# A macaron block: the route stage's row maxima, low parts and normalising are moved between engines and places

## The chip, the cores and the metric

The kernel runs on one core of one Trainium2 chip. A core has TensorE (PE: matrix products, transposes as products with an identity), VectorE (DVE), ScalarE (ACT), GpSimd (POOL) and SyncE (SP), which issues the DMAs. Each engine works through its own list of instructions in order, and semaphores tie the lists together. The metric is the time of one execution in microseconds (us) on the device. Before the change the median of 3 runs is 1989.15 us (1987.82 to 1989.57).

## The reference

The block is ffn, attention, ffn. Each ffn is a soft mixture of experts; its first part, the route, is what the change touches:

```python
x = L0_attn_x                                   # (4, 2048, 256)
x = x + 0.5 * ffn(layernorm(x))
x = x + attention(layernorm(x))
x = x + 0.5 * ffn(layernorm(x))

def ffn(x, ...):                                # E, S = 16, 64 -> 1024 slots
    x = layernorm(x) * g + b
    se = layernorm(slot_embeds) * scale
    logits = einsum('bnd,esd->bnes', x, se)
    dispatch = softmax(logits, axis=1)          # over the tokens
    combine = softmax(logits over all slots)    # over experts and slots
    slots = einsum('bnd,bnes->besd', x, dispatch)
    ... experts (gate, up, down), then combine @ eout
```

## The kernel before

There are three stages per ffn, each with its own names in the profile: route (f1r, f2r), experts (f1e, f2e) and combine (f1c, f2c); attention (at) stands between the two ffns. The banks of PSUM are f1bank and f2bank.

The route works by batches (4), each of four groups of 512 tokens (four tiles of 128); the 1024 slots are eight chunks of 128, or two halves of 512. A product in full precision is made of three products of high and low parts, so a token tile, its transpose and the exponentials are each split into `hi` (a copy that rounds) and `lo` (the difference).

`emit(b, fill, drain)` writes the work of one batch for one engine. Fill is for batch b: token statistics (VectorE), normalising (GpSimd, line 380), the transposes of the tokens (TensorE, line 681, "T"), their high parts (ScalarE, line 587) and low parts (VectorE, line 444), the logits as eight chunks of six matmuls (lines 692 to 694, `mm(0)` to `mm(7)`), their eviction with a bias (ScalarE, line 596), the maximum of each slot over tokens (VectorE, line 466), the maximum of each token over chunks (lines 459 and 456), and its last step, the transposes of that row maximum (TensorE, line 701) with a reduction (line 479). Drain is for batch b − 1: the exponentials (ScalarE, line 601; they need the maxima of the whole batch), their transposes (TensorE, line 707), their high parts (ScalarE, line 659) and low parts (VectorE, line 485), the token parts (GpSimd, lines 389 and 391), and the dispatch matmuls, twelve a tile (lines 733, 734 and 737, "D(0)" to "D(3)"), which add up in four banks over the batch. At the end of its last group VectorE scales these four banks (line 575) by the inverse sums of the exponentials. The inverse sums are made in that group (lines 506 and 508), stored to memory by SP (line 352) and loaded back as a row in every partition (line 355); only then can the scaling start. SP also stores the normalised tokens (line 311).

`batches` runs `emit` for batch 0 with fill alone, in a loop for batches 1 and 2 with both, once more for batch 3 with both, and at last with drain alone. No scheduler moves anything: the order on each engine is that of the code. PSUM has two banks for logits (`ps_l`), two for transposes (`ps_t`) and four for the dispatch (`ps_s`). In batch 0 the transposes of a group's row maxima stand behind chunk 0 of the next group; in later batches they stand at the end of their own group.

## Time and profile before

| | |
|---|---|
| median of 3 runs | 1989.15 us |
| profiled execution | 1985.45 us, of which the span on the core 1983.4 |
| mean granted clock of TensorE | 0.976 |
| TensorE busy | 1827.8 us (92%), 11720 instructions |
| VectorE busy | 1340.6 us (68%) |
| ScalarE busy | 1089.3 us (55%) |
| GpSimd busy | 895.2 us (45%) |

The first route begins at about 50 us and its last drain ends at about 500; the second stands where attention has ended, from 1169 on. A row's start is in microseconds from the start of the span. Square brackets at the end of a row give the idle time of the engine before it and which instruction ended it. A clock of 1.00 is 2.4 GHz and 0.50 is 1.2 GHz.

### The profile page before, as it was taken

Reading aid. Unit: us, or ns where it says so; the run is one execution under the profiler, and the core shown is the slowest. Engines: PE = TensorE matmul, PEld = TensorE weight load, DVE = VectorE, ACT = ScalarE, POOL = GpSimd, SP = SyncE. Lnnn points to the kernel's source line nnn. Section 1 sums busy time; section 2 is a strip of 40 time slices with the busy share of each in tenths; the row PEclk is TensorE's granted clock in tenths of the full one; section 3 lists DMA queues with packets and bytes.
Section 4 is the critical chain, followed back from the end, with each engine's and each line's share of the span. In section 5 each row is a group of like instructions: output and inputs, shape, how many; then the busy total and the mean of one; then the engine's idle time right before and its main releaser. Section 6 shows DMA issues by size and latency. Waiting matters only on the chain. (4 is left out here: it accounts for less than half of the span.)

```text
span 1983.4 us, 35336 instructions
## 1 busy us (share of the span) xinstructions
PE 1827.8 (92%) x11720; PEld 1633.2 (82%) x11720; DVE 1340.6 (68%) x2421; ACT 1089.3 (55%) x2146; POOL 895.2 (45%) x1029
## 2 busy tenths in 40 slices
PE   1889999999999899959999968999999999989999
PEld 1778787878899899958999956888878789989998
DVE  5775666554688888835555458666665548888886
ACT  1465556556555677724444325556655655557775
POOL 1454544414666455412222226446443346655553
PEclk9999999999999999979999989999999899999999
DMA  2553334322465577721222145333332426546774
GB/s 65 185 197 126 120 148 148 128 104 99 136 228 173 175 257 264 261 74 54 74 63 63 43 147 213 135 111 149 145 141 107 148 56 216 188 156 234 256 261 164
DMA packets 106670, 298.25 MB, mean 150 GB/s; under 512 B 16256, under 2 KB 56320, under 8 KB 94272
## 3 DMA queue, kind: packets, MB, share of 16 engines
q1 hardware_dynamic: 106560, 296.88, 42.1%
q8 instruction: 57, 0.93, 0.2%
q14 instruction: 53, 0.43, 0.1%
HBM read 187.63 MB, written 109.22 MB: 150 GB/s over the span
## 5 line engine op out<-in xcount | busy, mean ns | idle before, releaser
L115 POOL TENSOR_TENSOR pool_carrier<-minus_half 128x1 f32<-128x1 f32 x236 | 76.3, 323 | 565.4 <-PE f2bank L737 133.0
L596 ACT ACTIVATE f1r_lt<-f1bank,slot_shift 128x512 f32<-128x512 f32 x128 | 88.1, 688 | 171.2 <-PE f1bank L694 171.2
L596 ACT ACTIVATE f2r_lt<-f2bank,slot_shift 128x512 f32<-128x512 f32 x128 | 88.2, 689 | 170.6 <-PE f2bank L694 170.6
L485 DVE TENSOR_TENSOR f1r_e_lo<-f1bank,f1r_e_hi 128x512 fp32r<-128x512 f32 x128 | 82.6, 685 | 91.7 <-ACT f1r_e_hi L659 91.1
L485 DVE TENSOR_TENSOR f2r_e_lo<-f2bank,f2r_e_hi 128x512 fp32r<-128x512 f32 x128 | 82.7, 685 | 91.5 <-ACT f2r_e_hi L659 90.9
L1333 PE MATMUL f2bank<-f2c_eo,f2c_e_hi 128*128 128x258 f32 (+1 forms) x512 | 131.5, 288 | 3.5 <-DVE f2c_eo L1250 3.4
L1333 PE MATMUL f1bank<-f1c_eo,f1c_e_hi 128*128 128x258 f32 (+1 forms) x512 | 130.8, 287 | 3.7 <-DVE f1c_eo L1250 3.4
L1334 PE MATMUL f2bank<-f2c_eo,f2c_e_hi 128*128 128x256 f32 (+1 forms) x512 | 129.6, 284 | 0.0
L1334 PE MATMUL f1bank<-f1c_eo,f1c_e_hi 128*128 128x256 f32 (+1 forms) x512 | 128.9, 283 | 0.0
L1205 POOL TENSOR_TENSOR f2c_e_lo<-f2c_lt,f2c_e_hi 128x512 fp32r<-128x512 f32 x64 | 83.0, 1297 | 91.9 <-ACT f2c_e_hi L1304 91.8
L1205 POOL TENSOR_TENSOR f1c_e_lo<-f1c_lt,f1c_e_hi 128x512 fp32r<-128x512 f32 x64 | 83.1, 1298 | 90.8 <-ACT f1c_e_hi L1304 90.7
L692 PE MATMUL f1bank<-f1r_xT_hi,emb_hi 128*128 128x512 f32 x256 | 105.0, 410 | 1.5 <-DVE f1r_xT_lo L444 1.4
L692 PE MATMUL f2bank<-f2r_xT_hi,emb_hi 128*128 128x512 f32 x256 | 105.1, 410 | 1.4 <-DVE f2r_xT_lo L444 1.4
L1552 POOL TENSOR_TENSOR at_base<-at_xin,at_xn 128x1024 f32<-128x1024 f32 x16 | 38.2, 2390 | 150.8 <-DVE at_xout L1615 147.8
L1333 PEld LDWEIGHTS f2bank<-f2c_eo,f2c_e_hi 128*128 128x128 f32 x512 | 98.4, 192 | 7.8 <-issue 5.1
L1333 PEld LDWEIGHTS f1bank<-f1c_eo,f1c_e_hi 128*128 128x128 f32 x512 | 97.5, 191 | 8.3 <-issue 5.1
L733 PE MATMUL f2bank<-f2r_e_hi,f2r_xs_hi 128*128 128x512 f32 x252 | 104.0, 413 | 0.0
L733 PE MATMUL f1bank<-f1r_e_hi,f1r_xs_hi 128*128 128x512 f32 x252 | 103.7, 412 | 0.0
L694 PE MATMUL f1bank<-f1r_xT_hi,emb_lo 128*128 128x512 f32 x256 | 101.3, 396 | 0.0
L694 PE MATMUL f2bank<-f2r_xT_hi,emb_lo 128*128 128x512 f32 x256 | 101.2, 395 | 0.0
L693 PE MATMUL f1bank<-f1r_xT_lo,emb_hi 128*128 128x512 f32 x256 | 100.7, 393 | 0.0
L693 PE MATMUL f2bank<-f2r_xT_lo,emb_hi 128*128 128x512 f32 x256 | 100.7, 393 | 0.0
(321 smaller groups left out, 6611.7 us busy)
## 6 DMA issues: line engine op xcount, KB each, us to landing
logits<-f1r_lt SPq DMA_DIRECT2D x16, 2048.0 KB, 7.3
f1c_lt<-logits SPq DMA_DIRECT2D x32, 1024.0 KB, 7.1
logits<-f2r_lt SPq DMA_DIRECT2D x16, 2048.0 KB, 7.3
f2c_lt<-logits SPq DMA_DIRECT2D x32, 1024.0 KB, 7.1
f1r_xin<-in_L_attn_x SPq DMA_DIRECT2D x16, 512.0 KB, 4.8
normalized<-f1r_xin SPq DMA_DIRECT2D x16, 512.0 KB, 2.7
f1r_xback<-normalized SPq DMA_DIRECT2D x16, 512.0 KB, 8.1
f1e_raw_g<-in_L_ffn_Wg SPq DMA_DIRECT2D x16, 512.0 KB, 4.1
```

Of the source, the lines that this page charges most:

```text
L115: pool.tensor_tensor(c["pool_carrier"][:, col:col + 1], c["minus_half"][:, 0:1], c["minus_half"][:, 0:1], ALU.add)
L485: dve.tensor_tensor(e_lo[t % 2][:, h * BANK:(h + 1) * BANK], ps_t[h][:, :], rd(e_hi[t % 2][:, h * BANK:(h + 1) * BANK]), ALU.subtract).the ...
L596: act.activation(lt[:, g, sc, :], ps_l[sc % 2][:, :], ACT.Identity, bias=c["slot_shift"][:, sc:sc + 1]).then_inc(logit_out, 1)
L692: pe.matmul(ps_l[sc % 2][:, :], c["emb_hi"][:, k, cols], xT_hi[par][:, k, :], start=k == 0, stop=False)
L693: pe.matmul(ps_l[sc % 2][:, :], c["emb_hi"][:, k, cols], xT_lo[par][:, k, :], start=False, stop=False)
L694: mm = pe.matmul(ps_l[sc % 2][:, :], c["emb_lo"][:, k, cols], xT_hi[par][:, k, :], start=False, stop=k == KD - 1)
L733: pe.matmul(ps_s[k * HB + h][:, :], xs_hi[t % 2][:, cols], e_hi[t % 2][:, half], start=start, stop=False)
L1205: pool.tensor_tensor(e_lo[:, sc, :], lt[par][:, sc, :], rd(e_hi[:, sc, :]), ALU.subtract).then_inc(lo_by_pool, 1)
L1333: pe.matmul(ps_y[t][:, 0:LO], e_hi[:, sc, tile], eo[:, bpar, sc, 0:LO], start=sc == 0, stop=False)
L1334: return pe.matmul(ps_y[t][:, 0:D], e_hi[:, sc, tile], eo[:, bpar, sc, LO:W], start=False, stop=False)
L1552: pool.tensor_tensor(base[q][:, :, :], xin[q][:, :, :], xn[q][:, :, :], ALU.add).then_inc(base_done, 1)
```

## The change

- In batch 0, and for group 0 of every later batch, the low parts of the transposed tokens are made by GpSimd. It can't read PSUM, so ScalarE copies the transposes to SBUF as well (`xT`).
- The tokens of groups 2 and 3 of batch 0 and of groups 0 and 1 of every later batch are normalised by ScalarE, one operation per tile (groups 0 and 1 of a batch belong to the work of groups 2 and 3 of the batch ahead), x times `rstd` plus an offset, which GpSimd prepares (`norm_offset`). SP's store of the normalised tokens then waits for ScalarE.
- The transposes of the row maxima of a group in batch 0 stand behind chunk 1 of the next group. Those of a batch's last group stand behind chunk 0 of the next batch, and those of batch 3 inside the last drain.
- In the last group of a batch chunks 6 and 7 both follow D(1), the last slot maxima go ahead of the last low part, and the first exponentials of the next drain are made there; the token parts of its first two tiles too.
- The dispatch is written by halves of the slots: both dims of the first half, then of the second. VectorE scales the first half while TensorE does the second. In the last drain the first dispatch is begun by halves, between those of the next transposes.

Its core as a diff (what is left out follows from it: semaphores, counts, the body of `dispatch_half`, the order of the maxima of pairs 0 and 1):

```diff
+    def pool_makes_lo(b, g):
+        return (isinstance(b, int) and b == 0) or g == NG - 1
+    def act_normalizes(b, g):
+        return (isinstance(b, int) and b == 0) or g >= NG - 2
...
-        def store_xn(i, par):
-            sp.wait_ge(xn_done, i + 1)
+        def store_xn(i, par, b, g):
+            wait_normalized(sp, i, b, g)
             sp.dma_start(xn_dram[i], xin[par][:, :, :]).then_inc(xn_stored[par], DMA)
...
+        def norm_offset(i, par, count):
+            pool.tensor_scalar(minus_mean[par][:, :], mv[par][:, :, 0], -1.0, 0.0, ALU.mult, ALU.add).then_inc(minus_done, 1)
+            pool.wait_ge(rstd_done, i + 1)
+            pool.wait_ge(minus_done, count)
+            pool.tensor_tensor(offset[par][:, :], minus_mean[par][:, :], rstd[par][:, :], ALU.mult).then_inc(offset_done, 1)
...
+        def transposed_lo(i, par):
+            for k in range(KD):
+                pool.wait_ge(xT_hi_done, KD * i + k + 1)
+                pool.tensor_tensor(xT_lo[par][:, k, :], xT[:, k, :], rd(xT_hi[par][:, k, :]),
+                                   ALU.subtract).then_inc(lo_by_pool, 1)
...
-                if drain:
+                if drain and g > 0:
                     token_parts(j, g % 2, 0)
                     token_parts(j, g % 2, 1)
+                if fill and exists(b, g, 1) and pool_makes_lo(b, g) and not first:
+                    transposed_lo(i + 1, (g + 1) % 2)
...
+                if first:
+                    transposed_lo(i + 1, (g + 1) % 2)
...
+                if fill and g == NG - 1:
+                    token_parts(j + 1, 0, 0)
+                    token_parts(j + 1, 0, 1)
...
+                if drain and fill and g == 0:
+                    tile(0)
+                elif drain and g == 0:
+                    exp_lo(j, 0, 1)
                 if nxt2:
                     token_stats(i + 2, g % 2)
...
                 tile(2)
-                maxima(2)
-                tile(3)
-                if drain and not fill and g == NG - 2:
-                    inverse_sums(b, j + 1)
-                maxima(3)
-                if fill and (drain or g == NG - 1):
+                over_tokens(2)
+                over_slots(2)
+                if drain and g == NG - 1:
+                    over_tokens(3)
+                    tile(3)
+                    over_slots(3)
...
+                else:
+                    tile(3)
+                    if drain and not fill and g == NG - 2:
+                        inverse_sums(b, j + 1)
+                    over_slots(3)
+                    over_tokens(3)
+                if fill and exists(b, g, 1) and (drain or g == NG - 1):
                     row_max(g, b, i)
                 if drain:
                     if g == NG - 1:
...
                         dve.wait_ge(inv_loaded, DMA * b)
                         for h in range(HB):
...
+                            if h == 0 and fill and not exists(b, g, 1):
+                                exp_lo(j + 1, 0, 0)
...
+            if keep:
+                act.activation(xT[:, k, :], ps_t[k][:, :], ACT.Copy).then_inc(xT_out, 1)
...
+        def normalize(b, g, par, tiles=range(GT)):
+            if exists(b, g, 2) and act_normalizes(b, g):
+                for t in tiles:
+                    if t == 0:
+                        act.wait_ge(offset_done, by_act(b, g))
+                    last = act.activation(xin[par][:, t, :], xin[par][:, t, :], ACT.Identity, bias=offset[par][:, t:t + 1],
+                                          scale=rstd[par][:, t:t + 1])
+                if t == GT - 1:
+                    last.then_inc(xn_by_act, 1)
...
+                def next_batch(*chunks):
+                    if fill and g == NG - 1:
+                        if 0 in chunks:
+                            act.wait_ge(tsum_done, b + 1)
+                            if exists(b, g, 1):
+                                act.wait_ge(e_tr, 1 + HB * GT * b * NG)
+                            else:
+                                act.wait_ge(lt_stored[0], DMA * B)
+                            act.wait_ge(max_done, 2 * b + 1)
+                        exponentials(0, exists(b, g, 1), chunks)
+                ending = fill and not exists(b, g, 1)
...
+                        else:
+                            evict(*((3, 4), (5,), (6, 7) if g == NG - 1 else (6,), ())[t])
+                            if fill and t == 1:
+                                normalize(b, g, g % 2)
+                            if t == GT - 1:
+                                next_batch(0, 1, 2, 3)
...
+        def dispatch_half(b, g, j, t, h):
...
+            if h == HB - 1:
+                mm.then_inc(dispatched, 1)
+            elif stop:
+                mm.then_inc(first_half, 1)
+        def dispatch(b, g, j, t):
+            pe.wait_ge(xs_done, 1 + GT * j + t + 1)
+            for h in range(HB):
+                dispatch_half(b, g, j, t, h)
...
-                late = fill and not drain and g > 0
+                late = fill and not begin and (not drain or g == 0)
                 mm(0)
                 if late:
-                    transpose_row_max(i - 1)
-                    mm(1)
+                    if not drain:
+                        mm(1)
+                    transpose_row_max(i - 1, ps_t[0])
+                    mm(1 if drain else 2)
+                    if not drain:
+                        mm(3)
                 if nxt:
...
+                if drain and fill:
+                    if g == 0:
+                        mm(3)
+                    if nxt and pool_makes_lo(b, g):
+                        pe.wait_ge(xT_hi_done, KD * (i + 2))
+                    elif nxt:
+                        wait_lo(pe, b, g + 1)
...
+                    for h in range(HB):
+                        pe.wait_ge(exp_done, NSC * j + HALF * (h + 1))
+                        transpose_exp(j, g, 0, fill, (h,))
+                    if g > 0:
+                        mm(3)
+                elif drain and g == 0:
+                    pe.wait_ge(exp_done, NSC * (j + 1))
+                    transpose_exp(j, g, 0, fill, (1,))
+                elif not late:
                     mm(3)
                 mm(4)
                 for t in range(GT):
-                    if drain:
+                    if drain and not fill and g == 0 and t == 0:
+                        pe.wait_ge(xs_done, 1 + GT * j + 1)
+                        for h in range(HB):
+                            dispatch_half(b, g, j, 0, h)
+                            transpose_exp(j, g, 1, False, (h,))
+                        transpose_row_max(i - 1, ps_l[0])
+                    elif drain:
                         pe.wait_ge(e_lo_done, 1 + HB * (GT * j + t + 1))
...
+                        elif g == NG - 1 and not nxt and fill:
+                            pe.wait_ge(exp_done, NSC * (j + 1) + HALF)
+                            transpose_exp(j + 1, 0, 0, False, (0,))
+                        dispatch(b, g, j, t)
+                    if not drain or g < NG - 1:
+                        if t < NSC - 5:
+                            mm(5 + t)
+                    else:
+                        for sc in ((5,), (6, 7), (), ())[t]:
+                            mm(sc)
+                if fill and drain and g < NG - 1:
+                    transpose_row_max(i, ps_t[0])
```

How it moves instructions, as the two orders show it (line, operation, output and inputs by the names of the program, shape, what it waits for):

TensorE, the end of batch 0, before: chunk 7 of the last group, the four transposes of its row maxima (input `over_chunks`), then the loop's entry and its first wait, which is for the low parts (`xT_lo_done`).

```order
L692 MATMUL f1bank<-f1r_xT_hi_258,emb_hi 128x512
L693 MATMUL f1bank<-f1r_xT_lo_260,emb_hi 128x512
L694 MATMUL f1bank<-f1r_xT_hi_258,emb_lo 128x512
L701 MATMUL f1bank<-ident,f1r_over_chunks 128x128 [waits f1r_chunk_max,f1r_xT_lo_done]
L701 MATMUL f1bank<-ident,f1r_over_chunks 128x128 x3
L290 UNCONDITIONAL_BRANCH
L290 ISA
L689 ISA [waits f1r_xT_lo_done]
```

The same place after: the end of chunk 7, the loop's entry, chunk 0 of batch 1 and then the transposes.

```order
L816 MATMUL f1bank<-f1r_xT_hi_258,emb_lo 128x512
L296 UNCONDITIONAL_BRANCH
L296 ISA
L811 ISA [waits f1r_lo_by_pool]
L814 MATMUL f1bank<-f1r_xT_hi_257,emb_hi 128x512 [waits f1r_logit_out]
...
L821 REGISTER_ALU
L823 MATMUL f1bank<-ident,f1r_over_chunks 128x128 [waits f1r_chunk_max]
L823 MATMUL f1bank<-ident,f1r_over_chunks 128x128 x3
```

The transposes of the row maxima have moved from ahead of the loop to behind the first chunk of the next batch, and the wait for low parts is now one for GpSimd's.

TensorE, the start of the last drain, before: the end of D(3) of batch 3, the row maxima, the transposes of the exponentials (input `f1r_lt`) of tiles 0 and 1, and the first matmul of D(0) with its waits.

```order
L737 MATMUL f1bank<-f1r_e_hi_268,f1r_xs_lo_266 128x512 x2
L701 MATMUL f1bank<-ident,f1r_over_chunks 128x128 [waits f1r_chunk_max]
L701 MATMUL f1bank<-ident,f1r_over_chunks 128x128 x3
L707 MATMUL f1bank<-ident,f1r_lt 128x128 [waits f1r_e_lo_done,f1r_row_max_done,f1r_exp_done]
L707 MATMUL f1bank<-ident,f1r_lt 128x128 x7
L707 MATMUL f1bank<-ident,f1r_lt 128x128 [waits f1r_e_lo_done]
L707 MATMUL f1bank<-ident,f1r_lt 128x128 x7
L733 MATMUL f1bank<-f1r_e_hi_267,f1r_xs_hi_263 128x512 [waits f1r_e_lo_done,f1r_xs_done,f1r_scaled]
```

The same place after, from the half transpose ahead of D(3) of batch 3 on (the rest of D(3) is left out).

```order
L829 MATMUL f1bank<-ident,f1r_lt 128x128 [waits f1r_exp_done,f1r_e_lo_done]
L829 MATMUL f1bank<-ident,f1r_lt 128x128 x3
L843 MATMUL f1bank<-f1r_e_hi_268,f1r_xs_hi_264 128x512 [waits f1r_e_lo_done,f1r_xs_done]
...
L845 MATMUL f1bank<-f1r_e_hi_268,f1r_xs_lo_266 128x512
L829 MATMUL f1bank<-ident,f1r_lt 128x128 [waits f1r_exp_done]
L829 MATMUL f1bank<-ident,f1r_lt 128x128 x3
L843 MATMUL f1bank<-f1r_e_hi_267,f1r_xs_hi_263 128x512 [waits f1r_e_lo_done,f1r_scaled,f1r_xs_done]
...
L845 MATMUL f1bank<-f1r_e_hi_267,f1r_xs_lo_265 128x512
L829 MATMUL f1bank<-ident,f1r_lt 128x128 x4
L843 MATMUL f1bank<-f1r_e_hi_267,f1r_xs_hi_263 128x512 [waits f1r_e_lo_done,f1r_scaled]
```

A half of tile 0's transposes has moved ahead of the last dispatch, and the first dispatch's halves alternate with the other half transposes; the row maxima come behind them.

SP, the last group inside the loop, before: the load of later tokens, the store of the normalised ones, then the store and the load of the inverse sums.

```order
L307 DMA f1r_xin_254<-in_L_attn_x 128x1024
L311 DMA normalized<-f1r_xin_255 128x1024 [waits f1r_xn_done]
L352 DMA inverse<-f1r_inv 128x8x1 [waits f1r_inv_done]
L354 REGISTER_ALU
L355 DMA f1r_inv_rows<-inverse 128x1024 [waits f1r_inv_stored]
```

The same place after.

```order
L343 DMA f1r_xin_254<-in_L_attn_x 128x1024
L326 REGISTER_ALU
L347 DMA normalized<-f1r_xin_255 128x1024 [waits f1r_xn_by_act]
L388 DMA inverse<-f1r_inv 128x8x1 [waits f1r_inv_done]
L390 REGISTER_ALU
L391 DMA f1r_inv_rows<-inverse 128x1024 [waits f1r_inv_stored]
```

Nothing has moved, but the store ahead of the inverse sums waits for ScalarE's normalising (`xn_by_act`) and no longer for GpSimd's (`xn_done`).

VectorE, from the last group of the loop to the first of the next turn, after: row maximum, the four scalings (line 653) with their waits, and then the low parts of the next group's tokens (line 505) behind them.

```order
L541 ISA [waits f1r_row_tr]
L541 TENSOR_REDUCE f1r_neg_row_max<-f1bank 128x4
L653 ISA [waits f1r_first_half,f1r_inv_loaded]
L653 SCALAR_TENSOR_TENSOR f1r_slots<-f1bank,gain,f1r_inv_rows 128x8x64
...
L653 ISA [waits f1r_dispatched]
L653 SCALAR_TENSOR_TENSOR f1r_slots<-f1bank,gain,f1r_inv_rows 128x8x64
...
L505 TENSOR_TENSOR f1r_xT_lo_260<-f1bank,f1r_xT_hi_258 128x512 [waits f1r_xT_hi_done]
L504 REGISTER_ALU
L505 TENSOR_TENSOR f1r_xT_lo_260<-f1bank,f1r_xT_hi_258 128x512 [waits f1r_xT_hi_done]
```

Before, the scaling had one wait for both halves of the dispatch; the low parts stood behind it in the same way.

## Rows read from the trace of the kernel before

**Rows 1.** The page's busy times: microseconds, share of the span, instructions.

```profile
PE 1827.8 (92%) x11720; PEld 1633.2 (82%) x11720; DVE 1340.6 (68%) x2421; ACT 1089.3 (55%) x2146; POOL 895.2 (45%) x1029
```

**Rows 2.** TensorE's waits: who waits, for whom; us in total, times, longest.

```profile
PE f2bank L701 <- DVE f2r_over_chunks L456: 16.6, 13, 4.8
...
PE f1bank L701 <- DVE f1r_over_chunks L456: 16.6, 13, 4.8
```

**Rows 3.** TensorE's timeline, routes' transposes, experts' start: start, us, [idle before, releaser].

```profile
65.90 0.66 PE L701 MATMUL f1bank<-ident,f1r_over_chunks 128*128 128x128 f32 x4 [1.41 <-DVE f1r_over_chunks L456]
...
80.53 0.65 PE L701 MATMUL f1bank<-ident,f1r_over_chunks 128*128 128x128 f32 x4 [2.16 <-DVE f1r_over_chunks L456]
...
111.07 1.08 PE L701 MATMUL f1bank<-ident,f1r_over_chunks 128*128 128x128 f32 x4 [4.82 <-DVE f1r_over_chunks L456]
...
223.52 0.66 PE L701 MATMUL f1bank<-ident,f1r_over_chunks 128*128 128x128 f32 x4 [1.51 <-DVE f1r_over_chunks L456]
...
444.07 0.66 PE L701 MATMUL f1bank<-ident,f1r_over_chunks 128*128 128x128 f32 x4 [1.38 <-DVE f1r_over_chunks L456]
...
446.39 1.97 PE L707 MATMUL f1bank<-ident,f1r_lt 128*128 128x128 f32 x8 [1.66 <-ACT f1r_lt L601]
...
449.77 1.97 PE L707 MATMUL f1bank<-ident,f1r_lt 128*128 128x128 f32 x8 [1.41 <-DVE f1r_e_lo L485]
...
512.50 0.35 PE L1033 MATMUL f1bank<-f1e_in_hi,f1e_hi_g 128*128 128x256 f32 x1 [2.57 <-DVE f1e_in_lo L978]
```

**Rows 4.** Windows: length, busy time and count by engine, granted clock, DMA share, GB/s.

```profile
65.90:80.53 14.63, 12.47 (x60) 10.16 (x60) 12.82 (x21) 6.48 (x10) 8.00 (x8) 1.00 0.54 203
...
106.25:121.95 15.70, 10.86 (x51) 8.77 (x51) 10.82 (x21) 10.79 (x25) 8.99 (x13) 0.89 0.62 236
...
222.00:233.46 11.46, 9.68 (x52) 7.62 (x51) 10.19 (x22) 10.09 (x24) 7.26 (x13) 1.00 0.82 303
...
333.55:344.45 10.90, 9.34 (x50) 7.51 (x50) 9.96 (x22) 8.26 (x21) 6.82 (x12) 1.00 0.82 323
...
442.70:456.40 13.70, 9.26 (x33) 7.29 (x34) 7.37 (x11) 10.12 (x28) 6.53 (x10) 0.63 1.03 364
...
514.00:515.00 1.00, 1.00 (x6) 1.00 (x6) 1.00 (x1) 1.00 (x2) 0.10 (x1) 0.50 0.96 369
```

**Rows 5.** ScalarE's timeline, batch 0: one eviction of logits.

```profile
91.67 0.69 ACT L596 ACTIVATE f1r_lt<-f1bank,slot_shift 128x512 f32<-128x512 f32 x1 [0.67 <-PE f1bank L694]
```

**Rows 6.** VectorE's timeline, batch 0: the low parts.

```profile
69.20 1.29 DVE L444 TENSOR_TENSOR f1r_xT_lo<-f1bank,f1r_xT_hi 128x512 fp32r<-128x512 f32 x2 [1.62 <-ACT f1r_xT_hi L587]
```

**Rows 7.** Groups by line, GpSimd and ScalarE: busy us, mean ns, idle before.

```profile
L1205 POOL TENSOR_TENSOR f1c_e_lo<-f1c_lt,f1c_e_hi 128x512 fp32r<-128x512 f32 x64 | 83.1, 1298 | 90.8 <-ACT f1c_e_hi L1304 90.7
...
L951 ACT ACTIVATE f1e_gel<-f1bank,biases 128x256 f32<-128x256 f32 x64 | 26.8, 465 | 10.6 <-PE f1bank L1035 10.5
```

**Rows 8.** GpSimd's timeline: normalising in batch 0 and in batch 1.

```profile
74.13 6.48 POOL L380 TENSOR_SCALAR f1r_xin<-f1r_xin,f1r_mv,f1r_rstd 128x256 f32<-128x256 f32 x4
...
148.35 5.39 POOL L380 TENSOR_SCALAR f1r_xin<-f1r_xin,f1r_mv,f1r_rstd 128x256 f32<-128x256 f32 x4
```

**Rows 9.** One line's instructions, line 459: duration ns min/median/max, first and last start.

```profile
L459 DVE TENSOR_TENSOR f1r_over_chunks<-f1r_over_chunks,f1r_lt x32: 1209/1218/1396, 62.3 to 442.1; 128x1024 f32<-128x1024 f32 x32
```

**Rows 10.** Timelines at the end of batch 1: SP's queue, ScalarE, VectorE.

```profile
208.97 0.43 SPq L352 DMA_DIRECT2D inverse<-f1r_inv  x1
...
209.51 0.69 ACT L596 ACTIVATE f1r_lt<-f1bank,slot_shift 128x512 f32<-128x512 f32 x1 [3.32 <-PE f1bank L694]
...
220.21 0.33 SPq L355 DMA_DIRECT2D f1r_inv_rows<-inverse  x1
...
224.94 2.72 DVE L575 SCALAR_TENSOR_TENSOR f1r_slots<-f1bank,gain,f1r_inv_rows 128x512 f32 x4
```

**Rows 11.** Transfers of lines 352 (store of inverse sums) and 355 (load), to landing.

```profile
DMA to landing us min/median/max: 9.1/9.7/11.2
...
DMA to landing us min/median/max: 3.3/4.4/5.9
```

More of the change, by code:

```diff
@@ L320, in sp_program @@
         load_x(1, 1)
-        store_xn(0, 0)
+        store_xn(0, 0, 0, 0)
         sp.wait_ge(xT_tr, KD)
@@ L405, in emit @@
         def emit(b, fill, drain):
+            first = isinstance(b, int) and b == 0
             for g in range(NG):
```

216 lines of the change are left out of this document (111 added, 105 removed).

## The prediction

> **What bounds the kernel now.** I read the page's busy times first. TensorE is busy 92% of a span of 1983.4 us and VectorE 68% [rows 1], so a gain can only come from TensorE's idle time or from time at a low clock. The view of TensorE's waits comes next: outside start-up and attention the largest name in it is line 701, the transposes of the row maxima, with 13 waits and 16.6 us in each of the two routes; line 707, the transposes of the exponentials, adds 1.7 and 1.4 [rows 2]. The timeline places them. In batch 0 line 701 waits 1.41, 2.16 and (the third, the same row 14.63 us later) 2.16; at the boundary from batch 0 to 1 it waits 4.82, at the next two 1.51 each, at the start of the last drain 1.38, followed by 1.66 and 1.41 at line 707 [rows 3]. The other six are 0.27 each, one per inner group, and the change leaves them. Last comes the granted clock by windows: 1.00 around a 2.16 wait, 0.89 over the stretch with the 4.82, 0.63 over the whole start of the drain, and 0.50, which is the 1.2 GHz level, where the experts start behind a 2.57 wait [rows 4].
>
> TensorE's pace at the full clock: ScalarE's evictions in batch 0 follow each other 0.69 busy and 0.67 idle, so a logits chunk of six 512-column matmuls takes 1.36 [rows 5] and one such matmul 0.227; a dispatch of a tile (twelve) is then 2.73, eight 128-column transposes with their lead 0.9, the four of line 701 0.46 (the first's 0.66 less its overlap [rows 3]).
>
> **Batch 0.** A step is 14.63 us, of which TensorE needs 8 × 1.36 + 0.9 + 0.46 = 12.3. VectorE is busy 12.82 of it [rows 4] and carries a backlog: from 69.20, behind a wait of 1.62, it works without a gap up to the line 456 that releases TensorE at 80.53 [rows 3, 6]. The change takes the two low parts (1.29) off it and with them the 1.6 us in which it waits for their high parts; 11.5 remain at most. Now VectorE is idle when the last chunk comes. From the last logits matmul: handover 0.2, eviction 0.69 [rows 5], line 459 1.22 [rows 9], line 456 0.7 (0.93 beside GpSimd), together 2.85. The transposes now stand behind two chunks of the next step (2.72), so 0.15 is left of each wait. 5.73 − 3 × 0.15 = **5.3 saved**.
> What is late next is the low parts on GpSimd. Nothing of that form stands in the route, the nearest row is combine's 1.30 us per 128x512 [rows 7], so 2.6 for two, on an engine that loses the four normalising operations (6.48 [rows 8]). Token transposes end 6.8 into the step, ScalarE's four copies between its evictions end by 10.2, the last low part by 11.5, and the next step's logits start at 12.3: 0.8 of slack. From below the cost is nothing. From above: at 1.62 each, what GpSimd pays per operation at 74.13 [rows 8], the last one ends 0.3 later, still in time. I take nothing.
> Four of GpSimd's normalising operations take 6.48 in batch 0 and 5.39 at 148.35, and line 459, which reads two tiles in SBUF, takes between 1.21 and 1.40, median 1.22, the long ones beside them [rows 8, 9]: the two engines slow each other by a fifth. If line 459 held GpSimd back for its whole 1.40, the last low part would be 0.6 late; that is rival D. The Trainium skill, page "GPSIMD Engine Reference", section "Key points", says that GpSimd shares its SBUF interfaces with VectorE and contends with VectorE's operations that have two SBUF inputs, which speaks against this move. The trace agrees on the direction.
>
> **Boundary 0 to 1.** From 106.25 to 121.95, 15.7 us; the work in it is 9.1, the wait 4.82, the low clock some 1.5. The over-chunk maximum now goes ahead of the last slot maximum and the negative maximum (1.21 + 0.17), and the backlog of some 1.0 is gone: 4.82 becomes 2.4. Then small ones: the token transposes 0.2 (VectorE's queue of 1.21 + 0.17 + 0.68 against 0.46 + 1.36), the two halves of the exponentials 0.45 each. 9.1 + 3.5 + 0.15 = 12.75, so **2.95 saved**.
>
> **Boundaries 1 to 2 and 2 to 3.** 11.46 and 10.90 us now [rows 4]. The row-max transposes move behind chunk 0 of the next batch, whose 1.36 covers most of the 1.51, and the earlier maxima cover the rest. Each would be 9.8 (9.1 of work and 0.7 of small waits for exponentials), 2.7 saved together. But here the change adds a wait. In the last two groups ScalarE normalises. The eviction that it follows starts at 209.51 [rows 10]; four operations of 128x256 stand nowhere in SBUF-to-SBUF form on ScalarE. Bounds: 0.35 each (half of the 512-wide eviction's 0.69 [rows 5]) and 0.47 (the experts' gelu of 128x256, 0.465 [rows 7]); I take 0.4, and they end at about 211.8. SP's store of the normalised tokens waits for them, and queued behind it on SP is the store of the inverse sums, which goes at 208.97 today [rows 10] and then at about 212.15: **3.2 later**. Its load follows 11.24 later (208.97 to 220.21) and lands 4.4 after that (the load's median, [rows 11]). Today that makes 224.6, and VectorE's scaling starts at 224.94: hardly any slack. With the change it lands near 227.7, and the four scalings (2.72) end at 230.4. VectorE's low parts of the next group stand behind them (1.29, ends 231.7), and TensorE, which has chunks 0 to 3, the row maxima and the token transposes to do until 228.8, waits for these before the first transposes of exponentials: 2.8 us, 0.5 of which it would have waited there anyway. So 9.8 + 2.3 = 12.1 and 11.95 for the other, whose transfers I take at the medians, 9.7 and 4.4 [rows 11], and which so has some tenths of slack: the 2.7 turn into a **loss of 1.7**. Cheapest would be the least of both transfers, 9.1 + 3.3 [rows 11]; then nothing is lost, which is rival B.
> The 9.1 to 11.2 us of a 4 KB store are the trace's [rows 11]; what makes them long is not in it, and if it were the token store ahead, the pair moves together all the same. The Trainium skill, page "DMA: Bandwidth & Descriptors", section "Specifications", gives a first-byte latency of some 0.6 us for SP's path; by it both transfers would take 2 us at most (an estimate) and the inverse rows would be in time. Its section "Queues, rings and completion order" says that a completion lands only after every earlier write of that DMA engine, which would keep the lag behind the token store. The trace speaks against the first and not against the second.
> A wait of that length can also drop the clock: behind 2.57 at the experts it is 0.50, around 2.16 it stays 1.00 [rows 4]. Half the speed over some 1.6 us of work costs 1.6. I charge one of the two boundaries: **1.6**.
>
> **Start of the drain.** 442.70 to 456.40, 13.7 us for 5.0 of work. By the new order VectorE scales the first half while the last dispatch does its second (1.36), then makes the first low half (0.69), then scales the second half and makes its low part. Counted from the end of the last dispatch, the first half of the new dispatch can start at 0.9, the second at 3.0 (two scalings 1.36 and 0.69, handovers 0.2), and all of it ends by 5.6. If the clock stays low throughout as today, it is 5 more, 10.6. The gaps shrink below every gap of today's, so I take 7.0, which charges 1.4 for the clock: **6.7 saved**. The early exponentials of group 0, which end the 1.66 wait today, lie beside the last dispatch, where ScalarE has 3.3 us gaps [rows 10].
>
> **Not counted.** ScalarE's extra copies in batch 0: it is busy 6.48 of 14.63 [rows 4]. GpSimd's offset operations, 4 elements a row, 0.2 each, beside its power of 1.03. In the inner groups the high parts behind ScalarE's normalising have 0.5 to spare, the exponentials' low parts in the last group 0.2 to 0.3, the token parts of group 0 on GpSimd 0.6 at least. These are the thinnest covers: were all gone by as much again, it is about 1 us per boundary.
>
> **Sum.** Per route 5.3 + 2.95 − 1.7 − 1.6 + 6.7 = 11.65; both routes show the same 16.6 [rows 2], so 23.3. The profiled execution took 1985.45, 3.70 below the median of the runs shown. 1985.45 − 23.3 + 3.70 = 1965.85, 1966 in round numbers.
>
> **Rivals.**
> B: the inverse round trip is in time (store 9.1, load 3.3; or the tokens are normalised faster). For: the quicker ends of [rows 11]. Against: the medians add to 14.1, and this store took 11.24. Per route it gives back 1.7 + 2.7, the 1.6 of clock and, if the clock holds at the drain too, its 1.4: 2 × 7.4 = 14.8, 1951.
> C: the clock falls at both late boundaries and once more at 0 to 1. For: 0.89 over the 4.82's stretch, which is some 1.5 us. Against: 1.00 around 2.16. Two more at 1.6 per route, 6.4: 1972.
> D: batch 0 keeps its waits, because GpSimd's low parts, slowed by VectorE, end late and hold the logits. For: a fifth of mutual slowing. Against: 0.8 of slack. 5.3 twice is 10.6: 1976.6.
> E, the slower side: the inverse rows come much later still, because their store lands later behind the token store, at a DMA share of 0.82 around it [rows 4]. Everything of VectorE stands behind the scaling, and TensorE behind that. Each us beyond the slack costs one at four boundaries; the 23 saved are gone when they come 5.8 us later than I say, 8.6 late in all. Against: no store took over 11.2.
>
> **Chances.** Forecast 0.50, B 0.15, C 0.20, D 0.10, E 0.05. 0.2%, 4 us, is what a measurement of this kernel can tell from none. Forecast, B, C and D are all faster by more than that: with a little of D's spread, 0.93 faster, 0.03 same, 0.04 slower. The time is 1966. The range runs from B's 1951 to D's 1977: 1950 to 1977.
>
> **What would show it.** In TensorE's waits the row-max transposes drop from 16.6 to about 4.5 per route (2.4, and 0.15 and 0.27 pieces). A new wait of 2.3 to 3 for VectorE's low parts of tokens appears at two places per route, before the first transposes of exponentials. SP's inverse store comes about 3.2 us nearer to the end of its batch, and the scaling starts late by the same less the slack. The drain's start shows 7 us in place of 13.7 and a clock above 0.8. The forecast is wrong if the scaling isn't late (B), if the batch-0 step isn't about 12.4 (D), or if the windows behind the new waits stand near 0.5 at every boundary (C).

## The result and the profile after

The changed kernel takes 1970.49 us (median of 4 runs, 1964.36 to 1972.29) against 1989.36 (4 runs, 1987.82 to 1994.14): a ratio of 0.989, 95% interval 0.9872 to 0.9908, faster. Run again beside the first experiments it took 1968.99 against 1988.23 (0.9903, 0.9883 to 0.9923). The forecast was 1966, range 1950 to 1977. The profiled execution took 1972.29, its span is 1970.6.

TensorE's waits of the changed kernel, to be read against [rows 2]:

```profile
PE f1bank L829 <- DVE f1r_xT_lo L505: 5.6, 2, 3.1
PE f2bank L829 <- DVE f2r_xT_lo L505: 4.9, 3, 2.4
...
PE f1bank L823 <- DVE f1r_over_chunks L517: 4.3, 7, 2.7
PE f2bank L823 <- DVE f2r_over_chunks L517: 3.7, 7, 2.1
...
PE f2bank L843 <- DVE f2r_e_lo L547: 1.8, 3, 1.0
...
PE f2bank L814 <- ACT f2r_lt L688: 1.5, 1, 1.5
```

The waits for the row maxima (line 823, line 701 before) fell from 16.6 in each route to 4.3 and 3.7. In their place stands a wait for VectorE's low parts of tokens, 5.6 in the first route and 4.9 in the second, and one that was not forecast, for an eviction by ScalarE. TensorE's timeline, against [rows 3]: batch 0, the three boundaries, the start of the drain.

```profile
66.34 0.66 PE L823 MATMUL f1bank<-ident,f1r_over_chunks 128*128 128x128 f32 x4
78.88 0.66 PE L823 MATMUL f1bank<-ident,f1r_over_chunks 128*128 128x128 f32 x4
...
105.80 1.12 PE L823 MATMUL f1bank<-ident,f1r_over_chunks 128*128 128x128 f32 x4 [2.71 <-DVE f1r_over_chunks L517]
...
225.76 1.96 PE L829 MATMUL f1bank<-ident,f1r_et 128*128 128x128 f32 x8 [3.13 <-DVE f1r_xT_lo L505]
...
340.35 1.62 PE L829 MATMUL f1bank<-ident,f1r_et 128*128 128x128 f32 x8 [2.48 <-DVE f1r_xT_lo L505]
...
449.32 1.09 PE L829 MATMUL f1bank<-ident,f1r_lt 128*128 128x128 f32 x8 [0.98 <-DVE f1r_e_lo L547]
...
1339.03 1.09 PE L829 MATMUL f2bank<-ident,f2r_et 128*128 128x128 f32 x8 [2.33 <-DVE f2r_xT_lo L505]
```

And the windows that answer to [rows 4]: a step of batch 0, the boundaries 0 to 1, 1 to 2 and 2 to 3, and the drain's start (end of D(3) to the transposes of tile 2), all of the first route; the last two rows are the boundaries 0 to 1 and 1 to 2 of the second.

```profile
66.34:78.88 12.54, 12.49 (x61) 10.16 (x61) 12.16 (x19) 9.19 (x17) 4.59 (x7) 1.00 0.65 251
101.02:115.25 14.23, 11.06 (x51) 8.64 (x51) 7.79 (x11) 11.84 (x28) 3.66 (x6) 0.88 0.70 264
215.60:230.08 14.48, 11.35 (x52) 9.18 (x50) 7.00 (x13) 6.69 (x14) 5.33 (x7) 0.81 0.69 253
330.87:344.27 13.40, 10.91 (x51) 8.84 (x50) 6.93 (x13) 6.69 (x14) 5.33 (x7) 0.87 0.74 276
442.52:449.32 6.80, 5.03 (x30) 3.89 (x28) 4.62 (x9) 4.69 (x12) 6.38 (x10) 1.00 0.96 350
...
1214.22:1228.95 14.73, 10.46 (x51) 7.29 (x51) 7.19 (x11) 13.10 (x31) 2.99 (x5) 1.00 0.65 247
1329.69:1341.69 12.00, 9.49 (x51) 7.42 (x50) 5.96 (x10) 6.59 (x15) 5.33 (x7) 1.00 0.85 306
```

The step is 12.54 in place of 14.63, the start of the drain 6.80 in place of 13.7, at full clock. The boundaries 1 to 2 and 2 to 3 are longer than before, 14.48 and 13.40 against 11.46 and 10.90, and their clock is 0.81 and 0.87. In the second route the boundary 1 to 2 takes 12.00 at full clock; the last row of the timeline is its wait, and the eight transposes behind it take 1.09 us, where the same eight take 1.96 in the first route at the low clock. (A stretch that begins where a run of matmuls ends is cut 0.16 us earlier here than in [rows 4]. So each part below is good to 0.2 us; a whole route is not touched by it.)

Why VectorE's low parts are late, from three timelines at the end of batch 1 (against [rows 10]; here TensorE is 6.69 us earlier in the program than it was):

```profile
202.82 0.69 ACT L688 ACTIVATE f1r_lt<-f1bank,slot_shift 128x512 f32<-128x512 f32 x1 [3.32 <-PE f1bank L816]
203.41 2.07 ACT L676 ACTIVATE f1r_xin<-f1r_xin,f1r_offset,f1r_rstd 128x256 f32<-128x256 f32 x4
```

```profile
205.51 0.35 SPq L347 DMA_DIRECT2D normalized<-f1r_xin  x1
205.91 0.43 SPq L388 DMA_DIRECT2D inverse<-f1r_inv  x1
216.81 0.33 SPq L391 DMA_DIRECT2D f1r_inv_rows<-inverse  x1
```

```profile
200.87 0.20 DVE L570 RECIPROCAL f1r_inv<-f1r_tsum 128x8 f32<-128x8 f32 x1
...
221.71 2.73 DVE L653 SCALAR_TENSOR_TENSOR f1r_slots<-f1bank,gain,f1r_inv_rows 128x512 f32 x4 [3.27 <-DMA f1r_inv_rows<-inverse]
224.35 1.28 DVE L505 TENSOR_TENSOR f1r_xT_lo<-f1bank,f1r_xT_hi 128x512 fp32r<-128x512 f32 x2
```

Counted from the eviction, the inverse store was 0.54 ahead of it and is 3.09 behind: 3.6 later (forecast 3.2; a normalising operation takes 0.52 in a run of four, not 0.4). The inverse sums are ready at 201.07, but their store goes 4.8 us later, because it stands behind a token store that waits until ScalarE has normalised. The scaling waits 3.27 for the load, and the low parts, which TensorE wants, run behind it.

### The profile page after: what moved, and what is told of

Same layout as the page of the kernel before. It is cut to its first block and busy times, and to the rows that moved or that the text cites. A ratio compares the mean times of both kernels' runs of the same rounds, so it can differ in the third digit from the quotient of the medians.

```text
span 1970.6 us, 35473 instructions
## 1 busy us (share of the span) xinstructions
PE 1826.4 (93%) x11720; PEld 1632.3 (83%) x11720; DVE 1333.0 (68%) x2397; ACT 1128.0 (57%) x2233; POOL 830.8 (42%) x1005
## 5 line engine op out<-in xcount | busy, mean ns | idle before, releaser
L115 POOL TENSOR_TENSOR pool_carrier<-minus_half 128x1 f32<-128x1 f32 x220 | 59.3, 270 | 640.8 <-PE f1bank L845 165.7
```

The lines of the kernel that those rows point to most:

```text
L115: pool.tensor_tensor(c["pool_carrier"][:, col:col + 1], c["minus_half"][:, 0:1], c["minus_half"][:, 0:1], ALU.add)
```

## The experiments

All are made from the changed kernel; e1 to e10 are the names by which the expectations call them. The changed kernel itself ran again on the chip of e1, e2 and e6.

**The changed kernel again.** 

> The changed kernel once more, as the yardstick for the others on the same chip. Median about 1970.5 us, as measured before (1964.4 to 1972.3). Both theories: in each route two waits of TensorE of 2.3 to 3.1 us for VectorE's low parts of tokens, at the boundaries 1 to 2 and 2 to 3. Where the clock falls behind them or behind the 2.1 to 2.7 us wait at the boundary 0 to 1, a run is up to 2 us longer per place; that makes the spread of this kernel wider than that of the kernel before.


Measured: 1968.99 us (1968.70 to 1969.58), ratio 0.9903 (0.9883 to 0.9923). The waits for low parts are there (5.9 and 5.1 us in the two routes). The wider spread is not: these four runs lie within 0.9 us, the first four within 7.9. And the clock falls in other places. In the first route it stays high at all three boundaries, in the second it falls at the boundary 2 to 3; the eight transposes behind the waits of 3.03 and of 2.53 show it:

```profile
225.27 1.09 PE L829 MATMUL f1bank<-ident,f1r_et 128*128 128x128 f32 x8 [3.03 <-DVE f1r_xT_lo L505]
...
1446.51 1.97 PE L829 MATMUL f2bank<-ident,f2r_et 128*128 128x128 f32 x8 [2.53 <-DVE f2r_xT_lo L505]
```

The routes take 453.3 and 455.1 us here, 456.2 and 453.3 in the first profiled execution.

**e1, inverse store first.** On SP, lines 388 and 347 change places:

```diff
+                if drain and g == NG - 1:
+                    sp.wait_ge(inv_done, b)
+                    sp.dma_start(inv_dram..., inv...)
                 if fill and exists(b, g, 2):
                     store_xn(i + 2, ...)
-                if drain and g == NG - 1:
-                    sp.wait_ge(inv_done, b)
-                    sp.dma_start(inv_dram..., inv...)
```

> SP stores the inverse sums ahead of the normalised tokens; nothing else differs from the changed kernel. Theory A (the inverse rows are late because their store is queued on SP behind a store that waits for ScalarE, and VectorE's low parts are queued behind the scaling): the store goes at once when the sums are made, about 4.7 us earlier, the scaling no longer waits for the load, the four waits of TensorE (3.13 + 2.48 + 2.33 + 2.38 = 10.3 us) go and with them up to 4 us of low clock: 1957 to 1961 us. Rival R (the low parts are late because ScalarE, now with the normalising in its queue, makes the high parts late): the waits stay, 1969 to 1972. Of the transfer itself: if the token store ahead of it makes the inverse store's 9.7 us, it lands in under 5 us now; if the 4-byte elements do, it stays at 9 to 11.


Measured: 1955.69 us (1955.22 to 1957.64), ratio 0.9839 (0.9818 to 0.9859), 1.3 below the range of theory A. SP's queue and VectorE in it:

```profile
200.72 0.39 SPq L386 DMA_DIRECT2D inverse<-f1r_inv  x1
205.13 0.36 SPq L347 DMA_DIRECT2D normalized<-f1r_xin  x1
211.40 0.32 SPq L393 DMA_DIRECT2D f1r_inv_rows<-inverse  x1
```

```profile
217.36 0.69 DVE L543 TENSOR_REDUCE f1r_neg_row_max<-f1bank 128x512 f32 x1 [3.10 <-PE f1bank L825]
217.97 2.72 DVE L655 SCALAR_TENSOR_TENSOR f1r_slots<-f1bank,gain,f1r_inv_rows 128x512 f32 x4
```

The scaling starts with no wait, the four waits for low parts are gone, and so are 13.3 us: theory A, with its clock. But the load, which waits for the store, still goes 10.7 us behind it (10.9 in the changed kernel, 205.91 to 216.81): the token store ahead was not what made it long.

**e2, low parts first on VectorE**, SP unchanged:

```diff
                     row_max(g, b, i)
+                if fill and g == NG - 1 and exists(b, g, 2):
+                    for k in range(KD):
+                        transposed_lo(i + 2, 1, k)
                 if drain:
                     if g == NG - 1:      # the four scalings
```

(and without them at g = 0 of the next batch). 

> VectorE makes the low parts of the next batch's group 1 ahead of the four scalings and no longer behind them; SP is as in the changed kernel. Theory A: the scaling still waits some 3 us for the load of the inverse rows, but TensorE's four waits for low parts go; what is left is a wait of up to 0.5 us per boundary for the first low parts of exponentials behind the scaling. 1958 to 1963 us. Rival R (high parts late on ScalarE): 1969 to 1972, since the order on VectorE would not matter.


Measured: 1958.18 us (1957.49 to 1959.12), ratio 0.9849 (0.983 to 0.9869). VectorE at the same place:

```profile
220.39 1.29 DVE L505 TENSOR_TENSOR f1r_xT_lo<-f1bank,f1r_xT_hi 128x512 fp32r<-128x512 f32 x2 [2.13 <-ACT f1r_xT_hi L673]
221.59 2.72 DVE L657 SCALAR_TENSOR_TENSOR f1r_slots<-f1bank,gain,f1r_inv_rows 128x512 f32 x4
```

The scaling starts as late as in the changed kernel (221.59 against 221.71), and yet 10.8 us are gone: the late scaling itself costs little, what is queued behind it does. A little is left: TensorE's waits for the low parts of exponentials (line 833), which are still behind the scaling, are 2.7 us per route here and 1.6 in e1. With both edits, **e6**: 

> Both edits, SP's inverse store first and VectorE's low parts first. Theory A: the two remove the same wait, so together they give no more than the better one: 1956 to 1961 us, within 2 us of e1. If it were much less, each had removed another wait.


Measured: 1956.94 us (1954.59 to 1960.02), ratio 0.9842 (0.9818 to 0.9865), no different from the first alone: both remove the same wait.

**e3, GpSimd normalises group 1 again** (batch 0's turn included; `act_normalizes` is true for g < 3 in batch 0 and for g = 2 later). 

> The tokens of group 1 of every later batch are normalised by GpSimd again, in the last group of the batch ahead; the rest is the changed kernel (1968.99 us on this chip's last call). Theory A: SP's token store waits for GpSimd, which ends before ScalarE did, the inverse store goes about 3.6 us earlier, as in the kernel before, and of each of the four waits of 2.3 to 3.1 us at most 0.3 stays: 1957 to 1961 us, near the 1955.7 of the kernel whose SP stores the inverse sums first. Rival R: GpSimd, which now makes low parts and token parts in that group as well, pays 5.4 us for the four operations and hands over the token parts late: TensorE's dispatch waits for GpSimd there, and the time is 1962 to 1968.


Measured: 1959.49 us (1957.97 to 1960.85), ratio 0.9845 (0.9829 to 0.9862). The time is theory A's, and the four waits are gone, but a new one stands at the boundary 0 to 1, in a place that no expectation named:

```profile
PE f2bank L814 <- POOL f2r_xT_lo L447: 5.3, 1, 5.3
PE f1bank L814 <- POOL f1r_xT_lo L447: 5.0, 1, 5.0
```

```profile
96.14 6.13 POOL L423 TENSOR_SCALAR f1r_xin<-f1r_xin,f1r_mv,f1r_rstd 128x256 f32<-128x256 f32 x4
```

There GpSimd normalises for 6.13 us before it makes the low parts of batch 1's first group. In return the row maxima are in time there: their longest wait in the route is 0.3.

**e4, low parts of batch 0 on VectorE** (`pool_makes_lo` is true for g = 3 alone). 

> In batch 0 the low parts of groups 1 to 3 are made by VectorE from PSUM again; where TensorE has the transposes of tokens and row maxima, and ScalarE's normalising, is as in the changed kernel. Theory A (what makes the step 12.55 us in place of 14.63 is both, the low parts off VectorE and the later transposes): VectorE stops for the high parts in the middle of a step with its maxima queued behind, the row maxima are late again, the step is 13.5 to 15 us, and the two routes lose 6 to 14 us: 1975 to 1983. Rival (the place of the transposes alone does it, since it covers 1.36 us): the step stays under 13 us, 1969 to 1971.


Measured: 1987.18 us (1985.14 to 1988.63, 10 runs), ratio 0.9984 (0.9974 to 0.9994): 16 us lost by the ratios, outside what either theory gave. TensorE, VectorE and ScalarE in batch 0:

```profile
79.17 0.47 PE L814 MATMUL f1bank<-f1r_xT_hi,emb_hi 128*128 128x512 f32 x1 [3.07 <-ACT f1r_lt L688]
83.40 0.66 PE L823 MATMUL f1bank<-ident,f1r_over_chunks 128*128 128x128 f32 x4 [1.23 <-DVE f1r_over_chunks L517]
```

```profile
70.98 0.69 DVE L505 TENSOR_TENSOR f1r_xT_lo<-f1bank,f1r_xT_hi 128x512 fp32r<-128x512 f32 x1 [2.99 <-ACT f1r_xT_hi L669]
73.24 0.69 DVE L505 TENSOR_TENSOR f1r_xT_lo<-f1bank,f1r_xT_hi 128x512 fp32r<-128x512 f32 x1 [1.57 <-ACT f1r_xT_hi L669]
73.85 1.40 DVE L498 BATCH_NORM_STATS2 f1r_stats<-f1r_xin 128x6 f32<-128x256 f32 x4
```

```profile
77.85 0.60 ACT L676 ACTIVATE f1r_xin<-f1r_xin,f1r_offset,f1r_rstd 128x256 f32<-128x256 f32 x1 [3.74 <-POOL f1r_offset L418]
```

VectorE stands still for 4.56 us before the late high parts, with the statistics behind them; these give the offset, ScalarE waits 3.74 us for the offset before it normalises, and an eviction is queued behind that, for which TensorE waits 3.07 (my reading of the order; no run takes this chain apart). A step is 17.1 us, longer than the 14.63 of the kernel before. So with the rest of the change in place the low parts have to be off VectorE. It does not show how the gain of batch 0 divides: the larger wait here comes through ScalarE's normalising, and the later transposes without any offload, normalising included, were not run.

**e5, late exponentials at the last drain.** `next_batch` is left out for batch 3, and its four exponentials open the drain. 

> The first four exponentials of the last drain's group 0 are made at its start again, not beside the last dispatches of batch 3; the rest is the changed kernel. Theory A (the early exponentials carry about a third of the drain's 6.8 us gain): TensorE waits for them before the last dispatch, 2 to 4 us in each route, and ScalarE's queue behind is later: 1973 to 1977 us. Rival (the gain is of the halves alone; ScalarE has the time anyway): 1969 to 1971.


Measured: 1971.09 us (1970.46 to 1971.79), ratio 0.9902 (0.9886 to 0.9919), no difference from the changed kernel (0.9903) that the intervals show. Its trace has one wait of 1.0 us per route for ScalarE's exponentials; the part of each route from the first dispatch of batch 3 to the experts is 161.4 and 161.3 us, 160.4 and 161.1 in the changed kernel. The rival holds, to 1.0 us in the first route and 0.2 in the second.

**e8, inverse sums stored side by side.** This kernel is a probe and no candidate: it leaves out the right order of the sums, so the slots are scaled by wrong ones.

```diff
-                    sp.dma_start(inv_dram.rearrange("(c p a) -> p c a", p=P, a=1), inv[:, :].unsqueeze(2), ...)
+                    sp.dma_start(inv_dram.rearrange("(p c) -> p c", p=P), inv[:, :])
```

> The inverse sums are stored with a partition's eight values side by side (32 bytes) in place of eight single 4-byte elements 512 bytes apart; the row that is loaded back then holds them in another order than the slots, so the slots are scaled by the wrong sums. The order of SP is that of the changed kernel. With the store first it took as long as behind the token store, so the queue is not its cause. Theory F (the 1024 single elements are): it lands in 2 to 4 us, the scaling is in time, and the kernel takes what the one with the store first takes, 1955 to 1959 us. Rival G (a fixed latency of such a store to memory and of the wait on it): it stays above 8 us, 1968 to 1970.


Measured: 1954.36 us (1952.47 to 1956.23), ratio 0.9823 (0.9806 to 0.9839), 0.6 below the range of theory F. The store's transfer, against the first of [rows 11], and SP's queue:

```profile
DMA to landing us min/median/max: 1.4/1.9/2.4
```

```profile
205.43 0.42 SPq L388 DMA_DIRECT2D inverse<-f1r_inv  x1
207.87 0.32 SPq L390 DMA_DIRECT2D f1r_inv_rows<-inverse  x1
```

1.9 us in place of 9.7, behind the same token store, and the load goes 2.4 us behind it in place of 10.9. Theory F: the single elements make it long.

**e9, the drain's start in wholes.** In TensorE's order after D(3) of batch 3 (the half transposes ahead of D(3) go as well):

```diff
+                    transpose_row_max(i - 1, ps_l[0])
-                    transpose_exp(j, g, 0, fill, (1,))
+                    transpose_exp(j, g, 0, fill)
...
-                        for h in range(HB):
-                            dispatch_half(b, g, j, 0, h)
-                            transpose_exp(j, g, 1, False, (h,))
-                        transpose_row_max(i - 1, ps_l[0])
+                        transpose_exp(j, g, 1, False)
+                        dispatch(b, g, j, 0)
```

> TensorE starts the last drain in the order of the kernel before: after D(3) the row maxima (in the logits' bank), the whole transposes of tile 0, those of tile 1, and then D(0) in one piece. VectorE's and ScalarE's order stay as in the changed kernel, early exponentials too. Theory A (it is the order by halves that takes the start from 13.7 to 6.8 us): the first transposes wait for the row maxima, tile 1's for low parts behind a scaling, D(0) for the second scaling, the start is 10 to 13.7 us again and the clock falls in it: 3 to 7 us more per route, 1975 to 1983 us. Rival (the early exponentials and the earlier maxima did it): within 1 us per route, 1969 to 1971.


Measured: 1974.27 us (1970.61 to 1978.56), ratio 0.9904 (0.988 to 0.9928), between the two theories. The runs don't tell it from the changed kernel, the trace does: the start is 442.05 to 451.78, 9.7 us, between the changed kernel's 6.8 and the 13.7 of before.

```profile
442.05 0.60 PE L823 MATMUL f1bank<-ident,f1r_over_chunks 128*128 128x128 f32 x4
442.49 1.04 PE L829 MATMUL f1bank<-ident,f1r_lt 128*128 128x128 f32 x8
446.48 1.94 PE L829 MATMUL f1bank<-ident,f1r_lt 128*128 128x128 f32 x8 [2.95 <-DVE f1r_e_lo L547]
...
451.78 1.03 PE L829 MATMUL f1bank<-ident,f1r_lt 128*128 128x128 f32 x8
```

The new wait is 2.95 us, and the clock of the start is 0.82. The changed kernel has half a tile's transposes ahead of D(3); counted from the first dispatch of batch 3, which takes them in, it is 2.7 us shorter in the first route and 2.2 in the second. So the order by halves carries 2 to 3 of the 6.9 us. The other 4 are what this kernel keeps: the waits of 1.38 and 1.66 are zero here. That the earlier maxima and exponentials are the reason fits e5 only in part, where late exponentials cost a wait of 1.0; the maxima were not put back.

**e7, ScalarE's evictions first at the boundary 0 to 1**, on top of e1, with e1 again beside it:

```diff
-                    next_batch(0)
                     normalize(b, g, g % 2, (0,))
                     evict(NSC - 2)
-                    next_batch(1)
                     normalize(b, g, g % 2, (1,))
                     evict(NSC - 1)
+                    next_batch(0, 1)
```

> The kernel with SP's inverse store first once more, as the yardstick for the next one: 1955 to 1958 us.


1955.39 us (1954.66 to 1956.60), ratio 0.9811 (0.9795 to 0.9827).


> The inverse store first as in e1, and in batch 0's last group ScalarE evicts chunks 6 and 7 before it makes the first exponentials of the next drain. Theory A (at the boundary 0 to 1 TensorE waits 1.5 us in the second and 0.3 in the first route for an eviction that stands behind those exponentials, in the second behind a table load of 1.28 us too, and the row maxima are late by as much): these waits go and the one for the row maxima shrinks from 2.1 to 2.7 to about 1.5: 1 to 2 us less per route, 1952 to 1954. Rival (ScalarE's work there only changes places, and the transposes of exponentials wait for it as much): 1955 to 1957.


1955.50 us (1954.67 to 1956.40), ratio 0.9812 (0.9796 to 0.9829). The time is the rival's. In the first route the first dispatch comes 1.2 us earlier, in the second the wait of 1.4 goes, but waits of 0.8 and 0.3 for evictions come behind, and the dispatch is where it was (67.2 us into the route against 67.0).

**e10, GpSimd's low parts first**, with the edits of e1 and e3. 

> Inverse store first (as in e1), group 1 of every later batch normalised by GpSimd (as in e3), and in batch 0's last group GpSimd makes the low parts ahead of that normalising. Theory A (the 5.0 to 5.3 us wait of e3 at the boundary 0 to 1 is GpSimd's order, low parts behind 6.1 us of normalising, and ScalarE without normalising there lets the row maxima be in time): the wait of 5 us goes, the one for the row maxima stays at 0.3 or less, and a new one of up to 2.5 us for the normalised tokens of group 1 comes at the token transposes: 1952 to 1955 us, up to 3 below e1's 1955.4. Rival (the wait only changes its name, since GpSimd has 10 us of work in a stretch of 12 and hands over the token parts late): 1956 to 1960.


Measured: 1955.22 us (1953.46 to 1959.94), ratio 0.982 (0.9797 to 0.9843), between the two theories. The 5 us go, and 1.4 and 1.8 for row maxima and 2.6 and 0.5 for GpSimd's tokens come: no gain over the store first alone. That one, at 1955.4 to 1955.7, beats the kernel before and the changed one by moving one DMA.

## Why the prediction was right, point by point

- **Batch 0**, 5.3 per route: right. From 49.38 to 106.25 it took 56.87 us, now 49.26 to 101.02, 51.76: 5.1 less. The row-max transposes wait for nothing, where 0.15 each was forecast. What GpSimd's low parts cost VectorE was wrong (1.1 us a step, where a fifth of an operation was taken), and there was room for it: see the last section. (Two sums of this part are off by a little: 8 × 1.36 + 0.9 + 0.46 is 12.2 and 0.2 + 0.69 + 1.22 + 0.7 is 2.8. Neither moves the term.)
- **Boundary 0 to 1**, 2.95: the mis-sized term. The stretch went from 15.7 to 14.2 us in the first route and from 15.6 to 14.7 in the second: 1.5 and 0.8 saved. The wait for the row maxima is 2.71 and 2.10 against a forecast 2.4. In the first route what is missing is the clock: the forecast let the low clock of before go, but behind the 2.71 it fell again (0.88 over the stretch, 0.89 before), and from the transposes to the end of the next chunk it takes 3.19 us, where the second route at full clock takes 1.87: 1.3 us. In the second route it is an eviction, for which TensorE waits 1.53 (0.26 in the first). ScalarE makes the first exponential of the next drain ahead of two evictions, and in the second route a table load comes before it; the forecast put neither into its sum. (The 0.15 at the end of that sum stands for no row either.)
- **Boundaries 1 to 2 and 2 to 3**, a loss of 1.7 and 1.6 of clock: the mechanism was right in each link (SP's order, the scaling, the low parts behind it), and the waits of 3.13, 2.48, 2.33 and 2.38 are near the forecast 2.3 to 3. The sizes were not right. Taken from the end of one boundary to the end of the next, the two batches of the first route lost 3.3 and 3.2 us (111.51 to 114.83, 110.99 to 114.19), 6.5 against 3.3: the clock fell at both boundaries and not at one, as rival C had it. In the second route it fell at neither, and still they lost 1.5 and 1.6 (111.28 to 112.74, 110.99 to 112.57), 3.0 against a forecast 1.7 without the clock. Some 2 of these are the boundaries; most of the rest are waits of 0.52 and 0.28 ahead of them for the low parts of exponentials, whose cover the prediction called thin and did not count. The clock cost some 3.5 in one route and nothing in the other, where 1.6 was charged to each. So that the second route's loss comes out at 3.0 for 3.3 is luck, and so is which boundary pays: when the kernel ran again, one of these four fell, and it was another.
- **Start of the drain**, 6.7: measured 6.9. The forecast of 7.0 came from 5.6 and a charge for the clock; the clock stayed at 1.00, and two waits of 0.80 and 0.98 stand there instead. The saving is right; that the split came out to 0.2 us is luck.
- **Sum.** The routes went from 463.1 and 462.9 us to 456.2 and 453.3: 16.5 saved, not 23.3. Of the 6.8 that are missing, 3.6 are the boundaries 0 to 1 of both routes and 3.2 the later boundaries of the first. The medians differ by 18.9 us, and the time lies 4.5 above the forecast, inside its range. When the kernel ran again its routes saved 17.7. The rest of the program took 3.7 us more in this execution than in the one before, 2.6 of them in the first combine and 1.4 in attention, which the change does not touch; the profiled execution is also the slowest of its four.
- **Rivals.** B falls for the changed kernel, whose scaling waits 3.27 for the load; its case, the inverse rows in time, is made by the first experiment: 1955.7, where B said 1951. C holds for the first route of this execution and not for the second. D falls: TensorE waits for no low part of GpSimd's in batch 0. E falls: the store comes 3.6 us later, where 3.2 was forecast and E asks for 5.8 more.

## What to carry to other kernels

Before an operation moves to another engine, follow what is queued behind it on the engines that wait for it: here a 4 KB store stood behind a 512 KB one on SP, and through a scaling on VectorE it held TensorE, 13.3 us in the whole program. A transfer whose data are ready goes first on its queue. Where an engine's order can't be kept free of a late input, put what others need ahead of it, as the low parts ahead of the scaling.

## What the runs showed of the hardware

A store of 1024 single 4-byte elements took 9.7 us (median) with 512 KB ahead of it in SP's queue; with that store behind it (e1), what waits for it went 10.7 us after it, no earlier than the 10.9 before. The same 4 KB as 32 bytes a partition took 1.9 (e8). The prediction had cited the Trainium skill, page "DMA: Bandwidth & Descriptors", section "Queues, rings and completion order", by which a completion lands only after the earlier writes of that DMA engine. No trace here speaks against that, but it is not what makes this lag. The first-byte latency of some 0.6 us, which the section "Specifications" of that page of the Trainium skill gives, is nearer to what the store takes once the elements are side by side.

VectorE and GpSimd shut each other out, by more than the fifth of the prediction. In the changed kernel one VectorE operation with two inputs in SBUF, 1.22 us by itself, starts beside a GpSimd low part and takes 2.33:

```profile
71.88 2.33 DVE L520 TENSOR_TENSOR f1r_over_chunks<-f1r_lt 128x1024 f32<-128x1024 f32 x1
```

```profile
71.83 1.29 POOL L447 TENSOR_TENSOR f1r_xT_lo<-f1r_xT,f1r_xT_hi 128x512 fp32r<-128x512 f32 x1
```

The 1.1 us more are nearly the whole of GpSimd's 1.29. It is so in five of the six steps of batch 0 in the two routes; in the sixth VectorE takes 1.22 and GpSimd's first low part 2.42:

```profile
1197.62 1.22 DVE L520 TENSOR_TENSOR f2r_over_chunks<-f2r_lt 128x1024 f32<-128x1024 f32 x1
```

```profile
1197.58 3.67 POOL L447 TENSOR_TENSOR f2r_xT_lo<-f2r_xT,f2r_xT_hi 128x512 fp32r<-128x512 f32 x2
```

The Trainium skill, page "GPSIMD Engine Reference", section "Key points", names this contention for VectorE's instructions with two SBUF inputs; these rows agree and give its size. VectorE is busy 12.16 of 12.54 us in the step of 71.88, so the offload of 1.29 bought little of its time; what it bought, as I read it, is that VectorE no longer waits 1.6 us for the high parts.

TensorE's clock does not fall behind every wait of a length. In the first profiled execution of the changed kernel it fell behind 2.71, 3.13 and 2.48 in the first route and stayed behind 2.10, 2.33 and 2.38 in the second; when the same kernel ran again it stayed behind 2.71, 3.03, 2.68, 2.11 and 2.31 and fell behind 2.53. So no rule by the length of the wait comes out of these traces, and one execution doesn't show what the next one pays.

An ACT table load of 1.28 us stands ahead of the first early exponential at the boundary 0 to 1 of the second route; in the first route there is none at that place, and in the kernel before it came at 1223.42, behind the batch's evictions:

```profile
1212.68 1.28 ACT L693 ACT_TABLE_LOAD   x1
```
